# Four layer norms whose centring product takes the two terms of a residual sum one after the other, instead of the sum

## The reference

```
x = x + L0_conv(ln_c(x));   t = tokens(x); t = t + L0_ffn(ln_t(t)); x = image(t)
x = x + L1_conv(ln_c(x));   ...            t = t + L1_ffn(ln_t(t))
x = x + L2_conv(ln_c(x));   ...            t = t + L2_ffn(ln_t(t))
x = x + L3_conv(ln_c(x));   ...            t = t + L3_ffn(ln_t(t))

ln(v) = (v - mean(v)) / sqrt(var(v) + eps)                       over the channels
L0_ffn(x) = ln(mixture(x) + x) * gamma + beta                    two of 8 experts, weighted
L2_conv(x) = relu(batch_norm(conv_w @ [x, up(cH), up(cV), up(cD)]))
L1_ffn, L2_ffn, L3_ffn(x) = sum over the experts e of w[e] * (gelu(x @ W1[e] + b1[e]) @ W2[e] + b2[e])
```

## Time and profile before

| | us |
|---|---|
| median of 3 runs | 211.53 |
| lowest, highest | 211.3, 212.07 |
| the profiled execution's own time | 211.5 |
| its span | 209.7 |
| TensorE, VectorE, ScalarE, GpSimd busy in the span | 195.9, 124.5, 129.3, 42.5 |

### The profile page before, as it was taken

The page is one execution under the profiler, slowest core; times in us unless marked ns, Lnnn a source line. Parts: engine busy times, 40 slices in busy tenths (PEclk is TensorE's granted clock), DMA queues, the critical chain, the costliest instruction groups (busy, mean ns, idle before and its releaser), DMA issues.

```text
span 209.7 us, 3083 instructions
## 1 busy us (share of the span) xinstructions
PE 195.9 (93%) x1112; PEld 91.5 (44%) x1120; DVE 124.5 (59%) x364; ACT 129.3 (62%) x216; POOL 42.5 (20%) x60
## 2 busy tenths in 40 slices
PE   7998999999999998999999999999998997799993
PEld 2654222348876764322222363532234594333221
DVE  0466879957641824945342547595455688586435
ACT  2535688646355683776575830688685675598682
POOL 7761000000000000103963000100920011010740
PEclk9999999999999999999999999999999999999999
DMA  6999300000000000000000000000000000000001
GB/s 228 355 407 404 123 0 2 0 0 3 2 3 0 3 0 0 0 5 0 0 0 0 0 3 0 0 0 0 0 6 0 2 0 3 0 0 0 3 0 50
DMA packets 3119, 8.40 MB, mean 40 GB/s; under 512 B 550, under 2 KB 1072, under 8 KB 2976
## 3 DMA queue, kind: packets, MB, share of 16 engines
q1 hardware_dynamic: 2736, 7.60, 9.7%
q0 software_dynamic: 224, 0.46, 0.6%
q10 hardware_dynamic: 144, 0.13, 0.2%
HBM read 7.94 MB, written 0.26 MB: 39 GB/s over the span
## 4 chain that ended last, share of the span: by engine, by line
PE 78%; DVE 10%; ACT 8%; issue 3%; DVEq 0%; ACTq 0%
PE bank L362 17%; PE banks L379 9%; PE banks L291 8%; PE banks L380 7%; PE banks L555 6%; PE bank L302 5%; PE bank L296 4%; ACT hidden L727 3%; PE bank L343 3%; PE banks L516 2%; PE banks L497 2%; PE bank L612 2%; PE bank L480 2%; PE bank L325 2%; ACT rstd L689 1%
## 5 line engine op out<-in xcount | busy, mean ns | idle before, releaser
L727 ACT ACTIVATE hidden<-banks,pack_l 128x1024 f32<-128x1024 f32 (+1 forms) x43 | 44.9, 1052 | 18.3 <-PE banks L380 17.8
L362 PE MATMUL bank<-hidden,w 128*64 128x512 f32 (+1 forms) x160 | 41.4, 596 | 1.3 <-ACT hidden L727 1.3
L291 PE MATMUL banks<-idle_work 128*128 128x512 bf16 x116 | 31.1, 401 | 2.0 <-DVE idle_work L1000 1.2
L379 PE MATMUL banks<-split_x,w_hi 128*128 128x512 f16 x80 | 30.7, 384 | 0.0
L380 PE MATMUL banks<-split_x,w_lo 128*128 128x512 f16 x80 | 30.3, 379 | 0.0
L1442 POOL CAST split_x<-normed 64x256 f16<-64x256 f32 x8 | 4.0, 494 | 99.7 <-DVE normed L896 95.2
L685 ACT ACTIVATE squares<-bank 128x256 f32<-128x256 f32 x18 | 6.9, 383 | 22.5 <-PE bank L296 22.4
L379 PEld LDWEIGHTS banks<-split_x,w_hi 128*128 128x128 f16 x80 | 7.7, 97 | 28.4 <-issue 11.5
L291 PEld LDWEIGHTS banks<-idle_work 128*128 128x128 bf16 x123 | 12.4, 105 | 16.2 <-issue 5.0
L1451 POOL TENSOR_TENSOR total<-total,term 128x512 f32<-128x512 f32 x12 | 17.6, 1463 | 2.6 <-DVE term L982 2.0
L362 PEld LDWEIGHTS bank<-hidden,w 128*64 128x64 f32 x160 | 7.9, 134 | 18.3 <-issue 13.6
(11 more groups left out here) (314 smaller groups left out, 322.3 us busy)
## 6 DMA issues: line engine op xcount, KB each, us to landing
w_stage<-in_w SPq DMA_DIRECT2D x3, 512.0 KB, 13.2
w_stage<-in_w SPq DMA_DIRECT2D x1, 1024.0 KB, 9.6
conv<-in_conv SPq DMA_DIRECT2D x1, 800.0 KB, 7.7
w<-in_w SPq DMA_DIRECT2D x3, 256.0 KB, 13.4
w<-in_w SPq DMA_DIRECT2D x1, 512.0 KB, 10.4
toeplitz<-in_toeplitz SPq DMA_DIRECT2D x1, 512.0 KB, 11.2
gauss<-in_gauss SPq DMA_DIRECT2D x1, 512.0 KB, 12.4
pack_l<-in_pack_l SPq DMA_DIRECT2D x1, 373.5 KB, 14.9
```

The lines of the kernel that those rows point to most:

```text
L291: mm(out, idle_work[:, 0:128], idle_work[:, 0:cols], start=True, stop=True)
L362: last = mm(out[64 * h:64 * h + 64, cut], w2[l][:, (f * NE + e) * CH:(f * NE + e + 1) * CH], hidden[v % 3][:, h * 512 + cut.start:h * 512 ...
L379: mm(out, w1_hi[l][:, at:at + 128], split_x[h][:, :], start=True, stop=False)
L727: last = act(hidden[u % 3][:, cut], both[u % 2][:, cut], ACT.Gelu, bias=P(f"l{l}", "e_b1")[:, e * fc + f:e * fc + f + 1])
```

## The change

Centring is linear, so the centring product of a sum of two terms can be written as two products that accumulate in the same PSUM bank: the first (`center_first`, start=True, stop=False) takes the term that is there earlier, the second (`center_last`, start=False, stop=True) the later one. The residual sum itself is still formed, since later work reads it.

- **Norm 3**: VectorE writes `scaled2` = centred x gamma x rstd in one instruction for each chunk (L896 and L1116 go). TensorE takes x1_beta for both chunks, then scaled2. x[2] = scaled2 + x1_beta is formed by GpSimd, and read behind the convolution. The centred chunks of norm 3 go to banks 2 and 3, since banks 4 and 5 are being read.
- **Norms 5 and 7**: TensorE takes rest, then term[1], chunk after chunk (`norm_of_mixture`). VectorE does both last terms and then both sums; only in the last stage the order stays term 0, sum 0, term 1, sum 1.
- **Norm 6**: TensorE takes x[4] for both chunks, then relu of the batch norm. Of the 11 fillers 5 stand ahead of the products of x[4], and 2 behind them. ScalarE now does chunk 0 and VectorE chunk 1 (in two instructions), and the sums come after. The product of the statistics goes to bank 6.
- The counts of two semaphores (x_ready, ln_out) shift by what norms 2 and 3 no longer signal.

```diff
+        def centred(k, j):
+            return bank[(2 if k == 3 else 4) + j]
...
+            def center_first(k, j, src):
+                mm(centred(k, j)[:, 0:PIX], P("first", "center"), chunk(src, j), start=True, stop=False)
+
+            def center_last(k, j, src):
+                mm(centred(k, j)[:, 0:PIX], P("first", "center"), chunk(src, j), start=False, stop=True)\
+                    .then_inc(S["ln_centered"], 1)
+
+            def norm_of_mixture(k, l):
+                pe.wait_ge(S["moe_rest"], l)
+                center_first(k, 0, rest)
+                for j in range(INNER):
+                    pe.wait_ge(S["moe_last"], 2 * (l - 1) + j + 1)
+                    center_last(k, j, term[1])
+                    if j == 0:
+                        center_first(k, 1, rest)
+                averages(k)
...
             for j in range(INNER):
-                center(3, j, x[2], x_ready(2))
+                if j == 0:
+                    pe.wait_ge(S["l0_x1b"], 1)
+                    center_first(3, 0, x1_beta)
+                    center_first(3, 1, x1_beta)
+                pe.wait_ge(S["l0_scaled"], j + 1)
+                center_last(3, j, scaled2)
                 busy(2, bank[0][:, :])
                 average(3, j)
...
-            norm(5, x[4], x_ready(4))
+            norm_of_mixture(5, 1)
...
-            busy(11, bank[3][:, :])
-            norm(6, x[5], x_ready(5))
+            busy(5, bank[3][:, :])
+            pe.wait_ge(S["x_ready"], x_count(4, 1))
+            for j in range(INNER):
+                center_first(6, j, x[4])
+            busy(2, bank[3][:, :])
+            for j in range(INNER):
+                pe.wait_ge(S["bn_out"] if j == 0 else S["bn_out1"], 1)
+                center_last(6, j, bn_relu)
+            averages(6)
...
-            norm(7, x[6], x_ready(6))
+            norm_of_mixture(7, 2)
...
-            for j in range(INNER):
-                norm_chunk(2, j)
-                ve.wait_ge(S["ln_out"], 2 * 2 + j + 1)
-                STT(chunk(x[2], j), chunk(normed[2], j), P("l0", "gamma"), chunk(x1_beta, j), ALU.mult, ALU.add)\
-                    .then_inc(S["x_ready"], 1)
+            for j in range(INNER):
+                ve.wait_ge(S["ln_rstd"], 2 * 2 + j + 1)
+                STT(chunk(scaled2, j), centred(2, j)[:, 0:PIX], P("l0", "gamma"), chunk(rstd, j), ALU.mult, ALU.mult)\
+                    .then_inc(S["l0_scaled"], 1)
...
-            st.link(TS(chunk(bn_relu, 0), chunk(bn_in, 0), bn[:, 14:15], bn[:, 16:17], ALU.mult, ALU.add))
-            STT(chunk(x[5], 0), chunk(bn_relu, 0), 0.0, chunk(x[4], 0), ALU.max, ALU.add).then_inc(S["x_ready"], 1)
-            ve.wait_ge(S["bn_out"], 1)
-            TT(chunk(x[5], 1), chunk(bn_relu, 1), chunk(x[4], 1), ALU.add).then_inc(S["x_ready"], 1)
+            st.link(TS(chunk(bn_in, 1), chunk(bn_in, 1), bn[:, 14:15], bn[:, 16:17], ALU.mult, ALU.add))
+            TS(chunk(bn_relu, 1), chunk(bn_in, 1), 0.0, None, ALU.max).then_inc(S["bn_out1"], 1)
+            for j in range(INNER):
+                ve.wait_ge(S["bn_out1"] if j else S["bn_out"], 1)
+                TT(chunk(x[5], j), chunk(bn_relu, j), chunk(x[4], j), ALU.add).then_inc(S["x_ready"], 1)
...
+            po.wait_ge(S["l0_x1b"], 1)
+            for j in range(INNER):
+                po.wait_ge(S["l0_scaled"], j + 1)
+                G.tensor_tensor(chunk(x[2], j), chunk(scaled2, j), chunk(x1_beta, j), ALU.add).then_inc(S["x2_ready"], 1)
```

More of the change, by code:

```diff
@@ L295, in center @@
                 ready(j)
-                mm(bank[4 + j][:, 0:PIX], P("first", "center"), chunk(src, j), start=True, stop=True)\
+                mm(centred(k, j)[:, 0:PIX], P("first", "center"), chunk(src, j), start=True, stop=True)\
                     .then_inc(S["ln_centered"], 1)
+            def center_first(k, j, src):
[12 more added lines that the diff above has]
+                averages(k)
             def average(k, j):
@@ L684, in square @@
                 sc.wait_ge(S["ln_centered"], 2 * k + j + 1)
-                act(chunk(squares, j), bank[4 + j][:, 0:PIX], ACT.Square).then_inc(S["ln_squared"], 1)
+                act(chunk(squares, j), centred(k, j)[:, 0:PIX], ACT.Square).then_inc(S["ln_squared"], 1)
             def inverse_deviation(k, j):
@@ L895, in norm_chunk @@
                 ve.wait_ge(S["ln_rstd"], 2 * k + j + 1)
-                TT(chunk(normed[k], j), bank[4 + j][:, 0:PIX], chunk(rstd, j), ALU.mult).then_inc(S["ln_out"], 1)
+                TT(chunk(normed[k], j), centred(k, j)[:, 0:PIX], chunk(rstd, j), ALU.mult).then_inc(S["ln_out"], 1)
             def norm(k):
@@ L988, in experts, with last_term, whole @@
                 ve.wait_ge(S["moe_term"], terms)
-                st.mark(TT(rest[:, :], rest[:, :], term[(NE - 2) % 3][:, :], ALU.add))
+                TT(rest[:, :], rest[:, :], term[(NE - 2) % 3][:, :], ALU.add).then_inc(S["moe_rest"], 1)
                 ve.wait_ge(S["last_wide"], l)
-                for j in range(INNER):
[L992 to L997, removed]
-                    TT(chunk(x[2 * l + 2], j), chunk(term[1], j), chunk(rest, j), ALU.add).then_inc(S["x_ready"], 1)
+                def last_term(j):
+                    ve.wait_ge(*((S["moe_y"], base) if j else (S["moe_y_first"], l)))
+                    STT(chunk(term[1], j), chunk(last_y[j], j), P(f"l{l}", "e_b2")[:, NE - 1:NE],
+                        chunk(last_wide, j), ALU.add, ALU.mult).then_inc(S["moe_last"], 1)
+                def whole(j):
+                    ve.wait_ge(S["moe_rest"], l)
+                    ve.wait_ge(S["moe_last"], 2 * (l - 1) + j + 1)
+                    TT(chunk(x[2 * l + 2], j), chunk(term[1], j), chunk(rest, j), ALU.add).then_inc(S["x_ready"], 1)
+                last_term(0)
+                if l == 3:
+                    whole(0)
+                last_term(1)
+                if l < 3:
+                    whole(0)
+                whole(1)
             V.memset(idle_work[:, :], 0.0).then_inc(S["idle_work_zero"], 1)
```

43 lines of the change are left out of this document (23 added, 20 removed).

## The result

Before: 211.51 us, median of 20 runs (210.67 to 213.98). After: 212.28 us, median of 20 runs (211.31 to 212.89). The ratio is 1.0037, 95% interval 1.0023 to 1.0052: the change makes the kernel 0.8 us slower (0.5 to 1.1). The one execution of before at 213.98, over 1.5% above its fastest, is a slow one and not in the ratio. The forecast was 211.9, no difference beyond 0.5%.

A forecast was written before the change was run, and what follows sets the result against it. The kernel was taken as one long chain, 78% through TensorE, bound at each norm by what releases the centring product. Terms +0.28 + 0.65 - 0.15 - 0.42 = +0.36 us on 211.5 gave 211.9, range 210.7 to 212.9.

The forecast's parts named there:

- forecast class: Whole kernel: time within 0.5% of before, chance 0.76.
- the four terms: Norms 3, 5, 6 and 7: +0.28, +0.65, -0.15 and -0.42 us, together +0.36 us.
- norm 3: Norm 3: two first products stand ahead of the last product behind the fillers, square later by 0.28 us.
- norm 5: Norm 5: four products instead of two behind the fillers, second square and what follows 0.65 us later.
- norm 6: Norm 6: queue lets go at 132.37, neither relu is waited for, square 0.15 us earlier.
- norm 7: Norm 7: first product starts once rest is ready and the fillers end, square 0.42 us earlier.
- The rest I put at nothing: GpSimd's sums for x[2], last mixture's order, moved statistics product and shifted counts: no change in time.
- the prediction's lower bound: Norm 3: -0.46 us if the first products cost nothing.
- Rival 1: All four norms: added products cost nothing seen, each norm gains what VectorE gives up; -1.38 us, 210.1; chance 0.14.
- Rival 2: Centring bank's accumulating halves: weight loads not hidden, 0.11 us each for 16, 1.76 on top, 213.6; chance 0.10.

The follow-up runs named there:

- cut_before: Kernel before with nine fillers taken out (four of norm 2's tail, five at the end of the second mixture): 211.68 us, ratio 1.0006.
- n67_only: Kernel before with norms 6 and 7 alone changed, norms 3 and 5 and the last mixture as before: 211.64 us, ratio 0.9994.
- plain_waits2: Changed kernel, wait for x[2] moved ahead of the weight split, last mixture's waits as before: one profile, stretches of 70.14 and 45.25 us.
- cut_after: Changed kernel with four fillers of norm 2's tail and five at the end of the second mixture taken out: 211.17 us, ratio 0.9975.

## Why the prediction was right, and where it was short

**Right: the time, and the sign of no term was wrong.** Forecast 211.9 in 210.7 to 212.9, measured 212.28 (the runs of before had the median that the sum started from). The forecast class, within 0.5%, holds for the measured 0.37%, but the interval (0.23 to 0.52%) lies wholly on the slower side: this is a small real loss and not no difference, which a sum of +0.36 us said too, at half the size. Of the 0.42 us that the sum is short of the measured difference, 0.22 has a cause that the prediction left out; the four terms themselves came out to 0.01.

**Right: norm 3 (+0.28, measured +0.27) and norm 5 (+0.65, measured +0.65).** The mechanism was that TensorE's queue, not VectorE, decides there once the added products are in. The products stand back to back as forecast, and the filler experiments show it from both sides: in the changed kernel each of the nine fillers costs 0.19 to 0.21 us, in the kernel before none costs anything. One reading under it was too simple. The prediction calls VectorE's removed instruction at norm 5 hidden behind the fillers. That holds for chunk 0; chunk 1, on which the rest waits, was held by VectorE's sum (four records take 1.23 us in the earlier trace rows, 1.03 when back to back, and cut_before above). The sum had this right, since it counted from that product's measured end.

**Right: norm 6 (-0.15, measured -0.14) and norm 7 (-0.42, measured -0.42),** and neither a relu nor a last term came late. n67_only shows both apart from the rest.

**Wrong: "The rest I put at nothing".** It named GpSimd's sum, the last mixture's order, the moved statistics product and the counts. The work itself costs nothing, but two of these edits put a second semaphore ahead of an instruction that is on the chain. It cost 0.07 us at each of three places on the chain, +0.22 us in all, and plain_waits2 gave back all of it. With it the sum is +0.58. The step of the prediction that failed is that it weighed what each edit makes an engine do, and not what it makes an instruction wait for; "the last mixture keeps its order" was true and not enough.

The same count works the other way at norm 3: the first of norm 2's VectorE instructions waited for two semaphores before (rstd and VectorE's own chain), and started 0.58 us behind the start of 1/sqrt; it waits for one now, and starts 0.51 behind (42.24 to 42.75). It is another instruction now, but the kernel before holds the same comparison with one and the same instruction (the last section). In the changed kernel that is hidden by the queue. With the fillers cut it shows: norm 3 gained 0.53 us against before, where the prediction's lower bound was 0.46.

**Rival 1** (the added products cost nothing) fell: they are 0.43 us apart and the queue waits for them. Its gain, 1.38 us, is about what the four norms give once there is room for the products: 0.53 + 0.33 + 0.14 + 0.42 = 1.42 in cut_after. **Rival 2** (weight loads uncovered in the accumulating group) fell: in the changed kernel the four products of norm 5 start at 120.84, 121.27, 121.70 and 122.14. Here the measurement differs from the rule quoted from the Trainium skill ("TensorE: Matmul & The Clock Gate", Part 3, "The mechanism"): full-height weights load behind running products, 0.43 us for each product of two halves, accumulating in one bank or not.

**Left open.** The timed difference is 0.78 us and the trace's sum 0.58. The timing's interval holds both; no run was aimed at the rest. In the traces nothing else differs: ahead of norm 2 only the start does (the last section), and behind the last sum both kernels take 2.55 us. So a draw of later starts in the 20 executions of the changed kernel is what could fill it, and that is not shown.

## What to carry to other kernels

At the four norms here, splitting a product to start it earlier paid where TensorE had room for the part that is added, idle or with fillers that could go, and cost time where it had not. So count what stands in the queue ahead of the product, fillers too, before counting what the other engine saves. When work is taken off one engine's path, take the fillers off the other's in the same edit: here the change alone lost 0.8 us, nine fillers alone were worth nothing, and both together, with the plain waits and three more fillers cut, gained 1.4. Look at the granted clock of many executions when fillers go, not only at the profiled one. And a wait that is always satisfied is not free on a chain: where an instruction needs two events of the same engine, let one semaphore count both, or take the wait for the older event earlier, beside work that nobody waits for.

## What the runs showed of the hardware

**A second semaphore ahead of a VectorE instruction costs 0.07 us**, though it had long been satisfied, at all five places where it came or went (twice at the last sums, twice at the sums behind the tail, once at norm 2's). One trace shows it by itself. In the kernel before, norms 2 and 3 each have a first L896 with two semaphores to wait for (norm 3's waits for `borders_zero` too):

```profile
42.64 0.91 ACT L689 ACTIVATE rstd<-bank,pack_first 128x256 f32<-128x256 f32 x2 [0.36 <-PE bank L302]
...
46.13 0.47 ACT L689 ACTIVATE rstd<-bank,pack_first 128x256 f32<-128x256 f32 x1 [0.79 <-PE bank L302]
...
46.70 0.42 DVE L896 TENSOR_TENSOR normed<-bank,rstd 128x256 f32<-128x256 f32 x1 [1.69 <-ACT rstd L689]
```

They start 0.57 to 0.58 us behind the start of their 1/sqrt (42.64 to 43.22, 46.13 to 46.70). The L896 of norms 4 to 8 wait for one, and all ten start 0.51 behind it.

**The start is what spreads the times.** The first eleven fillers of an execution start 0.43 us apart at first, twice the 0.215 of later ones: the lower level of 1.2 GHz. At some moment, with TensorE at work since 1.19 us without a pause, the clock rises, and that moment is another in each execution: among the fillers in some, behind all eleven in others (in n67_only norm 0's four records still take 1.49 us where they take 1.03 at full clock). (The page's clock row reads full from the start and doesn't show it; the spacing does.) Before, as profiled, weight loads and then products, and behind it the kernel before with the nine fillers cut, whose first 40 us are the same program:

```profile
5.01 0.15 PEld L291 LDWEIGHTS banks<-idle_work 128*128 128x128 bf16 x1 [0.28 <-issue]
5.43 0.91 PEld L296 LDWEIGHTS bank<-x_in,pack_first 128*128 128x128 f32 x4 [0.28 <-issue]
```

```profile
5.71 1.03 PE L296 MATMUL bank<-x_in,pack_first 128*128 128x256 f32 x4
```

```profile
4.10 0.53 PEld L291 LDWEIGHTS banks<-idle_work 128*128 128x128 bf16 x3 [0.22 <-issue]
4.75 0.84 PEld L296 LDWEIGHTS bank<-x_in,pack_first 128*128 128x128 f32 x4
```

```profile
4.96 1.03 PE L296 MATMUL bank<-x_in,pack_first 128*128 128x256 f32 x4
```

In the first the loads are still 0.42 us apart at the eleventh filler (its load at 5.01, norm 0's first at 5.43), in the second three of them follow within 0.53 us from 4.10 on; norm 0's product starts at 5.71 and at 4.96. Over the nine profiled executions norm 2's first product starts between 40.07 and 41.44 us, and the distance from norm 0's first VectorE instruction to it is 33.23 to 33.25 in all of them. That is 1.4 us of spread that no edit has made, almost twice the effect under study, and the same as the timed executions of the kernel before at a clock of 1.0 have (210.73 to 212.09, 29 of them). The six at 0.992 or below, at 213.12 to 213.91, lie beyond that: a fall of the clock in mid-run, as in n67_only, is a second source. The sum of distances between events of one trace resolved 0.02 us where five rounds of timing resolved 0.6.
